# Scores of the second attention added onto the bank of two slots back by key differences

## What is computed

```python
xn = rms_norm(layernorm(x), gamma)
q, k, v = split(xn @ w_qkv)            # 16 heads, 64 channels each
sim = einsum('bhid,bhjd->bhij', q * 64 ** -0.5, k)
attn = softmax(sim, axis=-1)
out = einsum('bhij,bhjd->bhid', attn, v)
x = x + (out @ w_out) * silu(ffn(xn))
```

## Time and profile before

| | us |
|---|---|
| median of 3 runs | 1234.42 |
| lowest, highest | 1233.19, 1239.62 |
| the profiled execution | 1235.84 |
| its span, first to last instruction | 1234.0 |
| PE busy | 1177.2 (95%) |
| DVE busy | 850.5 (69%) |
| POOL busy | 755.4 (61%) |
| ACT busy | 576.3 (47%) |

### The profile page before, as it was taken

How to read it: one execution, slowest core, us unless ns; L and a number is a source line. 1 busy time by engine, 2 the same in 40 slices (tenths; PEclk the granted TensorE clock), 3 DMA queues, 4 the chain that set the end, 5 groups by cost and what they waited for, 6 DMA issues and landing times.

```text
span 1234.0 us, 22455 instructions
## 1 busy us (share of the span) xinstructions
PE 1177.2 (95%) x9276; PEld 771.4 (63%) x9276; DVE 850.5 (69%) x1062; ACT 576.3 (47%) x882; POOL 755.4 (61%) x487
## 2 busy tenths in 40 slices
PE   7999999998878999999999999999999999989997
PEld 6899999876654545555555555555555555447776
DVE  4665887566675587777777777778777777655543
ACT  1443344556535454544445445445454544544443
POOL 3565767753315577777777777787778787950000
PEclk9998999999989999999999999999999999989999
DMA  6000000020000020000000000000000000000000
GB/s 201 2 2 2 2 3 2 10 63 1 1 0 1 1 95 1 1 1 1 1 1 1 1 1 1 1 1 1 1 1 1 1 1 1 1 1 9 9 9 9
DMA packets 6981, 13.70 MB, mean 11 GB/s; under 512 B 1744, under 2 KB 4176, under 8 KB 6496
## 3 DMA queue, kind: packets, MB, share of 16 engines
q1 hardware_dynamic: 6096, 11.66, 2.8%
q10 hardware_dynamic: 784, 0.61, 0.3%
HBM read 11.22 MB, written 1.05 MB: 10 GB/s over the span
## 4 chain that ended last, share of the span: by engine, by line
PE 79%; DVE 11%; issue 3%; ACT 3%; POOL 3%; ACTq 1%; POOLq 0%; DVEq 0%
PE o_ps L1306 14%; PE mx_ps L1273 7%; PE ha_banks L494 6%; PE st_ps L1286 5%; PE st_ps L1288 5%; PE st_ps L1290 4%; PE st_ps L1292 4%; DVE mx_part L1463 3%; PE bank L1633 3%; PE bank L1635 3%; PE bank L1634 3%; PE pj_ps L1228 2%; POOL acc L1550 2%; PE pj_ps L1247 2%; PE pj_ps L1239 2%
## 5 line engine op out<-in xcount | busy, mean ns | idle before, releaser
L1550 POOL TENSOR_TENSOR acc<-acc,prob 128x1024 f32<-128x1024 f32 x192 | 467.0, 2432 | 127.2 <-ACT prob L1413 119.6
L1463 DVE TENSOR_REDUCE mx_part<-mx_ps 128x2 f32<-128x1024 f32 x251 | 307.3, 1224 | 127.0 <-PE mx_ps L1273 125.1
L1413 ACT ACTIVATE prob<-st_ps 128x1024 f32<-128x1024 f32 x256 | 248.8, 1024 | 211.5 <-PE st_ps L1292 211.5
L1306 PE MATMUL o_ps<-prob,v_cur 128*64 128x512 f32 x1024 | 247.7, 605 | 0.0
L1306 PEld LDWEIGHTS o_ps<-prob,v_cur 128*64 128x64 f32 x1024 | 66.6, 137 | 107.6 <-issue 104.5
L1481 DVE RECIPROCAL rden<-rden 128x128 f32<-128x128 f32 x128 | 120.2, 941 | 6.8 <-ACT rden L1383 6.8
L1273 PE MATMUL mx_ps<-k_hi,q_hi 64*128 64x512 f32 x502 | 112.3, 443 | 9.2 <-DVE mx_part L1463 8.8
L1273 PEld LDWEIGHTS mx_ps<-k_hi,q_hi 64*128 64x128 f32 x502 | 47.3, 184 | 104.4 <-issue 63.3
L1550 POOL TENSOR_TENSOR acc<-prob 128x1024 f32<-128x1024 f32 x32 | 75.9, 2371 | 54.7 <-ACT prob L1413 29.2
L1286 PE MATMUL st_ps<-q_hi,k_hi 64*128 64x512 f32 x512 | 101.7, 394 | 0.0
L1288 PE MATMUL st_ps<-q_lo,k_hi 64*128 64x512 f32 x512 | 101.1, 391 | 0.0
(11 more groups left out here) (351 smaller groups left out, 2088.2 us busy)
## 6 DMA issues: line engine op xcount, KB each, us to landing
h_w<-in_h SPq DMA_DIRECT2D x2, 1024.0 KB, 8.4
w_raw<-in_w SPq DMA_DIRECT2D x8, 192.0 KB, 3.4
x<-in_x SPq DMA_DIRECT2D x4, 256.0 KB, 7.8
head_wkv<-in_wkv SPq DMA_DIRECT2D x1, 1024.0 KB, 12.1
out<-fin SPq DMA_DIRECT2D x4, 256.0 KB, 2.2
m_w<-in_m SPq DMA_DIRECT2D x3, 256.0 KB, 3.0
sel_raw<-in_sel SPq DMA_DIRECT2D x1, 576.0 KB, 12.1
ha_head_pos<-in_pos ACTq DMA_DIRECT2D x2, 256.0 KB, 8.8
```

Source lines behind the costliest of these rows:

```text
L1306: mm = pe.matmul(o_ps[rows(h), :], v_cur[:, m % 2, j, rows(h)], prob[:, (16 * m + slot) % RING, h, :], start=(j == 0), stop=(j == KT - 1), ...
L1413: act.activation(prob[:, n % RING, :, :], st_ps[:, slot % 2, :, :], ACT.Exp, scale=SCALE).then_inc(s_exp, 1)
L1463: dve.reduce_max(mx_part[:, :, i, keys:keys + 1], maxima_banks(q, n), AX_X).then_inc(s_mxr, 1)
L1550: pool.tensor_tensor(total, old, new, ALU.add).then_inc(s_acc, 1)
```

## The change

In the first two slots of each half (key tiles 0 and 1) the scores are made as before, with `minus`·`q_max` now first. From the third slot on the bank isn't started anew: the slot adds onto what lies there from two slots back. Since the maximum is already in it, only the difference of the keys is needed, k[tile j] − k[tile j−2], split as `d_hi` + `d_lo`. Twelve slots of sixteen so have three pairs of matmuls in place of four. The waits of a slot are as before, but for one: slot 2 of a step waits for the last part of `d_lo`.

The differences are made once a step, out of the bank of the k units. ScalarE copies k unrounded into `k_all` (512 columns in the first half, 256 in the second), beside `k_hi`. VectorE subtracts it from the bank, shifted by two tiles, into `d_all`; it is still one 512-column unit of work, in two instructions in the first half. ScalarE rounds the 768 columns of `d_all` to `d_hi` in batch 5, and GpSimd subtracts these into `d_lo` ahead of slot 12. The first 256 columns of `d_lo` are the low part of k itself. The k units take the places of the q units in batches 0 and 4, and the q units those in batches 1 and 2; `k_all` takes room, and `early` begins 1 KB later.

```diff
+    TWO = 2 * P
-    QK = (("qk", 0, 0), ("qk", 1, 0), ("qk", 1, 1), ("qk", 0, 1))
+    QK = (("qk", 1, 0), ("qk", 0, 0), ("qk", 0, 1), ("qk", 1, 1))
+    SLOT_CUT = 12
...
         if u[0] == "qk":
-            pe.wait_ge(s_lo, 4 * q + QK.index(u) + 1)
+            _, t, half = u
+            pe.wait_ge(s_d if t else s_lo, 2 * q + half + 1)
...
+        if slot == 2:
+            pe.wait_ge(s_dlo, m + 1)
         if m or slot >= 2:
             pe.wait_ge(s_exp, 16 * m + slot - 1)
...
+        fresh = j < 2
+        if fresh:
+            for h in range(2):
+                pe.matmul(st[:, h, :], minus[rows(h), :], q_max[rows(h), half_of(half)], start=True, stop=True)
+        upper = kh[:, tile(j)] if fresh else dh[:, tile(j - 2)]
         for h in range(2):
-            pe.matmul(st[:, h, :], kh[rows(h), tile(j)], qh[rows(h), half_of(half)], start=True, stop=False)
+            pe.matmul(st[:, h, :], upper[rows(h), :], qh[rows(h), half_of(half)], start=False, stop=False,
+                      skip_group_check=True)
...
-            act.activation((k_hi if t else q_hi)[q % 2][:, half_of(half)], qk_bank(q, u), ACT.Copy).then_inc(s_hi, 1)
+            act.activation(k_hi[q % 2][:, half_of(half)], qk_bank(q, u), ACT.Copy).then_inc(s_khi, 1)
+            if q and half == 0:
+                act.wait_ge(s_d, 2 * q)
+            size = TWO if half else CH
+            act.activation(k_all[:, half * CH:half * CH + size], qk_bank(q, u)[:, 0:size], ACT.Copy).then_inc(s_kall, 1)
...
+    def scalar_differences(act, q):
+        act.wait_ge(s_d, 2 * q + 2)
+        act.activation(d_hi[q % 2][:, :], d_all[q % 2][:, TWO:], ACT.Copy).then_inc(s_dhi, 1)
...
+        if b == 5 and m + 1 < STEPS:
+            scalar_differences(act, m + 1)
...
+        elif half == 0:
+            dve.wait_ge(s_kall, 2 * q + 1)
+            dve.tensor_tensor(d_lo[q % 2][:, 0:TWO], whole[:, 0:TWO], k_hi[q % 2][:, 0:TWO].bitcast(F32), ALU.subtract)
+            dve.tensor_tensor(d_all[q % 2][:, TWO:CH], whole[:, TWO:], k_all[:, 0:TWO], ALU.subtract).then_inc(s_d, 1)
+        else:
+            dve.wait_ge(s_kall, 2 * q + 2)
+            dve.tensor_tensor(d_all[q % 2][:, CH:], whole, k_all[:, TWO:], ALU.subtract).then_inc(s_d, 1)
...
+    def gpsimd_cut(pool, q):
+        pool.wait_ge(s_dhi, q + 1)
+        pool.tensor_tensor(d_lo[q % 2][:, TWO:], d_all[q % 2][:, TWO:], d_hi[q % 2][:, :].bitcast(F32), ALU.subtract)\
+            .then_inc(s_dlo, 1)
```

More of the change, by code:

```diff
@@ L1083, in second_attention @@
     w_hi, w_lo = (pairs.sb(n, [P, PAIRS, W_QK], F32R) for n in ("w_hi", "w_lo"))
-    q_hi, q_lo, k_hi, k_lo = ([place.sb(n, [P, LEN], F32R) for place in (pairs, late)]
-                              for n in ("q_hi", "q_lo", "k_hi", "k_lo"))
+    TWO = 2 * P
+    q_hi, q_lo, k_hi, d_hi = ([place.sb(n, [P, size], F32R) for place in (pairs, late)]
+                              for n, size in (("q_hi", LEN), ("q_lo", LEN), ("k_hi", LEN), ("d_hi", LEN - TWO)))
+    d_all, d_lo = [], []
+    for place in (pairs, late):
+        d_all.append(Region(nc, place.at).sb("d_all", [P, LEN]))
+        d_lo.append(place.sb("d_lo", [P, LEN], F32R))
+    k_all = early.sb("k_all", [P, LEN - TWO])
     v_cur = late.sb("v_cur", [P, 2, KT, P])
@@ L1102, in second_attention @@
     s_mx, s_mxr, s_row, s_max = (at.sem(n) for n in ("s_mx", "s_mxr", "s_row", "s_max"))
-    s_hi, s_lo, s_v, s_den, s_osum, s_rcp, s_on, s_out = (
-        at.sem(n) for n in ("s_hi", "s_lo", "s_v", "s_den", "s_osum", "s_rcp", "s_on", "s_out"))
+    s_v, s_den, s_osum, s_rcp, s_on, s_out = (
+        at.sem(n) for n in ("s_v", "s_den", "s_osum", "s_rcp", "s_on", "s_out"))
+    s_qhi, s_lo, s_khi, s_kall, s_d = (at.sem(n) for n in ("s_qhi", "s_lo", "s_khi", "s_kall", "s_d"))
+    s_dhi, s_dlo = (at.sem(n) for n in ("s_dhi", "s_dlo"))
     BATCHES = 8
@@ L1283, in tensor_scores @@
         st = st_ps[:, slot % 2, :, :]
-        qh, ql, kh, kl = (t[m % 2] for t in (q_hi, q_lo, k_hi, k_lo))
+        qh, ql, kh, dh, dl = (t[m % 2] for t in (q_hi, q_lo, k_hi, d_hi, d_lo))
+        fresh = j < 2
[3 more added lines that the diff above has]
+        upper = kh[:, tile(j)] if fresh else dh[:, tile(j - 2)]
         for h in range(2):
-            pe.matmul(st[:, h, :], kh[rows(h), tile(j)], qh[rows(h), half_of(half)], start=True, stop=False)
+            pe.matmul(st[:, h, :], upper[rows(h), :], qh[rows(h), half_of(half)], start=False, stop=False,
+                      skip_group_check=True)
         for h in range(2):
-            pe.matmul(st[:, h, :], kh[rows(h), tile(j)], ql[rows(h), half_of(half)], start=False, stop=False)
+            pe.matmul(st[:, h, :], upper[rows(h), :], ql[rows(h), half_of(half)], start=False, stop=False,
+                      skip_group_check=True)
         for h in range(2):
-            pe.matmul(st[:, h, :], kl[rows(h), tile(j)], qh[rows(h), half_of(half)], start=False, stop=False)
-        for h in range(2):
-            mm = pe.matmul(st[:, h, :], minus[rows(h), :], q_max[rows(h), half_of(half)], start=False, stop=True)
+            mm = pe.matmul(st[:, h, :], dl[rows(h), tile(j)], qh[rows(h), half_of(half)], start=False, stop=True,
+                           skip_group_check=True)
         mm.then_inc(s_st, 1)
@@ L1358, in qk_bank @@
     def qk_bank(q, u):
-        return st_ps[:, 0, u[1], :] if q == 0 and u in QK[:2] else pj_ps[:, :]
+        return st_ps[:, 0, QK.index(u), :] if q == 0 and u in QK[:2] else pj_ps[:, :]
     def scalar_unit(act, q, u):
@@ L1436, in vector_low @@
         _, t, half = u
-        dve.wait_ge(s_hi, 4 * q + QK.index(u) + 1)
-        hi, lo = (part[q % 2][:, half_of(half)] for part in ((k_hi, k_lo) if t else (q_hi, q_lo)))
-        dve.tensor_tensor(lo, qk_bank(q, u), hi.bitcast(F32), ALU.subtract).then_inc(s_lo, 1)
+        whole = qk_bank(q, u)
+        if t == 0:
+            dve.wait_ge(s_qhi, 2 * q + half + 1)
+            dve.tensor_tensor(q_lo[q % 2][:, half_of(half)], whole, q_hi[q % 2][:, half_of(half)].bitcast(F32),
+                              ALU.subtract).then_inc(s_lo, 1)
+        elif half == 0:
[5 more added lines that the diff above has]
+            dve.tensor_tensor(d_all[q % 2][:, CH:], whole, k_all[:, TWO:], ALU.subtract).then_inc(s_d, 1)
     def vector_spread_max(dve, q, u):
```

40 lines of the change are left out of this document (25 added, 15 removed).

## The result

The changed kernel takes 1223.28 us (median of 9 runs, 1216.89 to 1228.62), the kernel before in the same session 1236.16 (9 runs, 1233.19 to 1239.91). The ratio is 0.9891, with a 95% interval of 0.9859 to 0.9924. In a later session it was 1219.93 against 1236.87, ratio 0.9872 (0.984 to 0.9904). So it is 1.1 to 1.3% faster, against a forecast of 1.3% and 1218.5 us.

A forecast was written before the change was run, and what follows sets the result against it. TensorE was taken to bound the middle steps and GpSimd the last. Gains of 15.8 (steps 1 to 14) and 0.5 (step 0), less 0.4 ahead, make 15.9 us: 1218.5 us, range 1212 to 1224 (62%), 8 in 10 within 1206 to 1228.

The forecast's parts named there:

- The bank of the maxima as the next bound: Batches 1, 2, 6, 7: second piece of maxima waits for the first's reduction, so 0.25 of 0.46 us gained each.
- Batch 3: Middle step: the turn of the maxima waits for VectorE's sum into y, so only 0.08 us is gained.
- Batch 5: Middle step: `k_all`, taken as 0.35 us, delays the reciprocal and the next reduction, leaving 0.05 us gained.
- The other prices: `d_hi` 0.8 us on ScalarE and the cut 1.8 us on GpSimd, both hidden in a middle step.
- the first `k_all`: Ahead of step 0, up to 0.60 us in ScalarE's row between the experts' last pieces: 0.4 us lost, an estimate.
- 14 steps (1 to 14) gain 15.8: Each of steps 1 to 14 gains 1.00 + 0.08 + 0.05 = 1.13 us, 15.8 together.
- VectorE slips behind GpSimd: Rival: `o_n` in batch 5 ends behind GpSimd's second addition, 1.7 us a step, 1242 us in all; 5% in full.
- Step 0: First step: batches gain 1.00 and 0.46 us, norm matmuls wait some 0.65 and 0.3 longer; net 0.5 gained.
- Step 15 and the end: Last step: GpSimd is full and TensorE waits longer than 3.56 us for its last addition; nothing gained.
- The clock as a rival: The granted clock falls behind new waits of TensorE; ten stretches losing 1.6 us each would eat the gain; 2%.

The follow-up runs named there:

- b_half: The kernel before, with VectorE's reduction of a piece of the maxima reading only 256 of the 512 keys: 1222.65 us, ratio 0.9889.
- a_half: The changed kernel, with VectorE's reduction of a piece of the maxima reading only 256 of the 512 keys: 1182.74 us, ratio 0.9564.
- a_zero: The changed kernel with a fourth pair of matmuls, of zero weights, put back in the twelve slots: 1236.09 us, ratio 0.9999.
- a_xrlo: The changed kernel with VectorE's product `xr_lo` moved from batch 2 to batch 5 of step 1: 1218.1 us, ratio 0.9851.
- after3: The changed kernel run once more, unaltered, in a later session: 1219.93 us, with a profiled span of 1214.7.
- a_noswap: The changed kernel with the q and k units back in their earlier order, k in batches 1 and 2: 1237.11 us, ratio 1.0009.

## Why the prediction held, point by point

**The bank of the maxima as the next bound: right.** A released piece came 1.82 behind the first and showed 0.50, as two pieces with nothing between them did in the earlier trace rows. Batches 1, 2, 6 and 7 gained 0.23, 0.25, 0.25 and 0.24, forecast 0.25 each. Batch 3 gained 0.07, forecast 0.08. Of the 2.76 us of matmuls 1.4 were held back, which `b_half` and `a_half` show by giving it back.

**Batch 5: mis-sized.** Forecast 0.05, measured 0.23, which is nearly the whole difference between 1.13 and the 1.28 a step that came. Its rows:

```profile
719.98 0.60 ACT L1402 ACTIVATE k_hi<-pj_ps 128x512 fp32r<-128x512 f32 x1
720.48 0.38 ACT L1407 ACTIVATE k_all<-pj_ps 128x256 f32<-128x256 f32 x1
720.88 0.69 DVE L1493 TENSOR_TENSOR d_all<-pj_ps,k_all 128x512 f32<-128x512 f32 x1 [0.57 <-ACT k_all L1407]
721.49 0.94 DVE L1535 RECIPROCAL rden<-rden 128x128 f32<-128x128 f32 x1
...
721.74 0.50 PE L1293 MATMUL mx_ps<-k_hi,q_hi 64*128 64x512 f32 x2
...
722.35 1.17 DVE L1517 TENSOR_REDUCE mx_part<-mx_ps 128x2 f32<-128x1024 f32 x1
```

`k_all` cost 0.38 as a row, near the 0.35 taken, but from copy to reciprocal only 1.51 − 1.24 = 0.27 were added (719.98 to 721.49, against 718.62 to 719.86 in the earlier trace rows). It starts 0.50 behind `k_hi`, whose row says 0.60. Likewise the reciprocal's follower starts 0.86 behind it, not 0.94, and a reduction that runs straight behind another instruction took 1.17, not 1.23. I had laid whole rows end to end, where instructions that follow each other overlap by about 0.1. The reduction so started 0.61 behind the batch's first piece, 0.07 later than the 0.54 of batch 2, and took 0.06 less, and the two cancelled.

**The other prices: right.** `d_hi` 0.84 (0.8 taken), the cut 1.81 to 1.82 (1.8), `k_all` of 512 columns 0.59 (0.60). `a_zero` shows them hidden. Ahead of step 0 the first `k_all` was put at 0.4 us, an estimate. From the last `su` row of the experts to the first turn before took 17.17 us, `a_xrlo` and `after3` 17.25, so it cost 0.1 at most. The Trainium skill, "ScalarE: Activation LUTs", section "What ACT_TABLE_LOAD costs", gives 186 ns + 0.833 ns a column for such a copy with immediate operands, which makes an estimate of 399 ns for 256 columns and 826 for 768. The rows, 0.38 and 0.84, agree to within 0.02 us.

**VectorE behind GpSimd: right for `o_n`, missed for `xr_lo`.** In batch 5 `o_n` took 1.81 in seven of the 13 middle steps where it had taken 1.80, and 2.0 to 2.3 in the others, without a cost, as the next reduction is due later. What the prediction took for slipping in between is more exact in single rows: the first of the two additions of the earlier trace rows ended at 725.38, not at the middle of the row, and `o_n` ended 0.55 behind it. It isn't that `o_n` needs a gap to hit; it ends 0.55 behind the addition it meets, whichever that is. I had considered the one place in a middle step and not step 1, where the normalisation puts another VectorE instruction with two SBUF operands 0.09 us ahead of an addition. The step of the prediction that failed is "14 steps (1 to 14) gain 15.8": step 1 lost 2.4 in the profiled run and 1.1 in `after3`. It gained 1.3 only with `xr_lo` moved. In the prediction's own terms this is the rival *VectorE slips behind GpSimd* come true, once, in an instruction that it didn't name.

**The exchange of units: not priced.** The prediction took it as given and went through the batches as they stood. `a_noswap` shows that without it the whole gain is gone. Nothing was wrong in the sum, but the margin of VectorE in batch 1 is small: in after `o_n` met the first of two additions 0.30 us before its end.

**Step 0: open to both sides.** Forecast 0.5 gained. Against the one trace of before (57.4) the changed kernel measured −2.1 and +2.7, and with `xr_lo` moved +2.7 and +0.8, with the step's granted clock at 0.83, 0.94, 0.94 and 0.88. The wait behind the k unit grew by 0.56, from 1.41 to 1.97, near the 0.65 that I had put on it. But in this step the clock moves more than any term, so the 0.5 is neither confirmed nor refuted.

**Step 15 and the end: right in kind.** Nothing was gained there; 1.1 lost in the profiled run, 0.3 of it ahead of the last `den`.

**The clock as a rival.** I gave 2% to a clock falling in the middle steps. It stayed at 1.00 there in every trace. But in the profiled run it was lower ahead of the attention (0.94 against 0.98), in step 0 (0.83 against 0.91) and in step 1 (0.96 against 1.00), and that goes with most of what the middle steps' gain lost there. The prediction had no term for it.

In sum, forecast 15.9: 13 middle steps gave 16.7 and not 14.7, step 1 took 2.4 and didn't give 1.1, step 0, the front and the end took the rest in this execution. In the quicker execution of `after3` the span fell by 19.3. The median lies between, and 1218.5 came near it in part by luck: the gain of a middle step was under-sized by a seventh, and a loss in step 1 wasn't seen. That 1223.28 lies inside the stated 1224 is luck too, as single runs scatter over 12 us with the clock. What was right on its merits is the middle step, 43.36 us where 43.5 was forecast, and the reason for it.

## What to carry to other kernels

Where the bounding engine waits for nothing, ask how far ahead the runner-up is at each handover: here the bank of the maxima was free only 0.41 us early, and so 0.25 of the 0.46 us taken out of a batch came in. Where a VectorE instruction with two SBUF operands starts within a tenth of a microsecond of a GpSimd addition, any edit that shifts the two can cost the addition's whole duration, also in a step that the edit doesn't mean to touch: list all such pairs, those of the first steps too. Chains on one engine are to be summed from start to start, since the rows overlap by about 0.1 us.

## What the runs showed of the hardware beyond that

- A 512-column VectorE product or difference with two SBUF operands that started while an addition of GpSimd ran ended 0.54 to 0.61 us behind that addition's end, nearly always 0.55, in all 13 traces. So it took what was left of the addition and 0.55: 2.79 us when it started 0.13 into it (`xr_lo` in after), 2.73 at 0.19 (`o_n` in `a_noswap`), 1.81 at 1.11 and 0.84 at 2.09 (`o_n` in batches 5 and 1 of after). Where it started first, by up to 0.09 us, it took 0.63 to 0.68 and the addition 2.75 to 2.91 in place of 2.4.
- A half-height pair of matmuls put behind a full-height unit starts 0.10 us later than a full-height one would (1.01 against 0.91), and a piece released by a reduction shows 0.50 and not 0.39.
- The same program took 361 to 367 us to the first turn and 54.7 to 59.5 us for step 0, with granted clocks of 0.94 and 0.83 in step 0, while its steps 2 to 14 agreed within 0.2 us of 564. From 100 to 110 us TensorE was busy throughout in both executions, at 0.66 in one and 1.00 in the other.
